# Paced loads, smaller |w| sums, one shift product per step and a reordered prologue in a kernel with a 256-step recurrence

## What is computed

```python
def cell(h, x):                              # scanned over the 256 steps
    gi = x @ W_ih + b_ih
    gh = h @ W_hh + b_hh
    r = sigmoid(i_r + h_r)
    z = sigmoid(i_z + h_z)
    n = tanh(i_n + r * h_n)
    return (1.0 - z) * n + z * h
...
x = x + moe(gru(cond, x))                    # 8 experts of 192, the best 2 per token
...
scale, shift = split(cond @ W_emb + b_emb)   # adaptation of the attention's input
xn = rms_norm(x, g) * (1.0 + scale) + shift
...
gamma = mean(abs(w))                         # of each of w1, w2, w3 (1408 x 512)
wq = clip(round(w / (gamma + eps)), -1, 1)
```

## Time and profile before

| what | value |
|---|---|
| median of 3 runs | 1829.79 us (1825.73 to 1830.11) |
| the profiled execution's own time | 1830.81 us |
| its span, first to last instruction | 1828.9 us |
| mean granted TensorE clock | 0.891 |
| TensorE busy (matmul) | 1611.4 us, 88% |
| VectorE busy | 1174.7 us, 64% |
| ScalarE busy | 916.3 us, 50% |
| GpSimd busy | 599.9 us, 33% |
| DMA moved | 90.36 MB |
| of it instructions, queues q8 and q14 | 3.83 MB in 234 packets, 0.66 MB in 81 |

### The profile page before, as it was taken

How to read it: one execution, slowest core, us unless ns; L and a number is a source line. 1 busy time by engine, 2 the same in 40 slices (tenths; PEclk the granted TensorE clock), 3 DMA queues, 4 the chain that set the end, 5 groups by cost and what they waited for, 6 DMA issues and landing times. The chain is left out here.

```text
span 1828.9 us, 77444 instructions
## 1 busy us (share of the span) xinstructions
PE 1611.4 (88%) x32043; PEld 1223.2 (67%) x32043; DVE 1174.7 (64%) x4229; ACT 916.3 (50%) x3325; POOL 599.9 (33%) x1805
## 2 busy tenths in 40 slices
PE   6999999999999999896299965788888888699999
PEld 5988999889999998896266532354545555444444
DVE  5777877777787788777644436566565666474231
ACT  5545555445455555545245445367666667532130
POOL 0333333323333333334345444133223223580000
PEclk9999999999999999555599985789888989699999
DMA  6010010200000001202446444000000000040001
GB/s 239 5 49 30 5 52 5 98 33 5 5 4 5 5 22 56 76 22 73 134 138 238 133 169 137 1 2 0 0 0 0 0 0 1 12 128 18 29 1 47
DMA packets 30635, 90.36 MB, mean 49 GB/s; under 512 B 4848, under 2 KB 6000, under 8 KB 30192
## 3 DMA queue, kind: packets, MB, share of 16 engines
q1 hardware_dynamic: 23920, 64.88, 10.4%
q0 software_dynamic: 6400, 20.98, 3.4%
HBM read 66.90 MB, written 18.87 MB: 47 GB/s over the span
## 5 line engine op out<-in xcount | busy, mean ns | idle before, releaser
L363 PE MATMUL bank<-arena 128*128 128x8 f16 x12288 | 500.9, 170 | 25.2 <-issue 14.0
L366 PE MATMUL bank<-arena 128*128 128x16 f16 x12288 | 495.2, 182 | 2.7 <-issue 2.1
L363 PEld LDWEIGHTS bank<-arena 128*128 128x128 f16 x12288 | 414.4, 97 | 57.9 <-ACT bank L459 32.0
L366 PEld LDWEIGHTS bank<-arena 128*128 128x128 f16 x12288 | 411.9, 97 | 4.1 <-issue 3.2
L635 POOL TENSOR_TENSOR arena<-arena 128x16 f32<-128x16 f32 x512 | 116.8, 228 | 565.9 <-DVE arena L566 551.2
L429 ACT ACTIVATE arena<-arena 128x16 f32<-128x16 f32 x512 | 114.4, 223 | 327.4 <-DVE arena L545 327.3
L545 DVE TENSOR_REDUCE arena<-bank 128x16 f32<-128x48 f32 x512 | 99.5, 194 | 105.2 <-PE bank L366 102.4
L556 DVE TENSOR_TENSOR_SCAN arena<-arena,bank 128x64 f32<-128x64 f32 x512 | 146.7, 287 | 21.0 <-ACT arena L429 6.9
L1898 PE MATMUL bank<-arena 128*128 128x512 f16 x704 | 152.3, 379 | 1.7 <-PEq L1419 1.7
L336 PE MATMUL bank<-arena 128*128 128x256 f16 x1008 | 150.4, 277 | 0.8 <-issue 0.7
L1454 PE MATMUL bank<-arena 128*128 128x512 f16 x576 | 144.4, 406 | 4.5 <-DVE arena L1698 4.5
(11 more groups left out here) (201 smaller groups left out, 2699.9 us busy)
## 6 DMA issues: line engine op xcount, KB each, us to landing
arena<-yrows SPq DMA_DIRECT2D x16, 512.0 KB, 4.1
arena<-in_wgu SPq DMA_DIRECT2D x8, 768.0 KB, 4.7
hrows<-arena SPq DMA_DIRECT2D x16, 256.0 KB, 4.1
arena<-in_xtok SPq DMA_DIRECT2D x16, 256.0 KB, 8.0
out_y<-arena SPq DMA_DIRECT2D x16, 256.0 KB, 2.0
arena<-in_wih SPq DMA_DIRECT2D x4, 768.0 KB, 7.5
arena<-in_whh SPq DMA_DIRECT2D x4, 768.0 KB, 5.3
arena<-in_xT SPq DMA_DIRECT2D x3, 1024.0 KB, 5.9
```

The costliest lines, as they stand in the source:

```text
L363: mm = nc.tensor.matmul(dst[:, j * B:(j + 1) * B, 1], w, h[:, 0], start=home not in opened, stop=False, skip_group_check=True)
L366: mm = nc.tensor.matmul(dst[:, j * B:(j + 1) * B, 1:3], w, h.rearrange("p a c -> p c a"), start=home not in opened, stop=False, skip_group ...
```

## The change

- SyncE's loads within the recurrence are cut: x in pieces of 128 KB (one k of one window of 32 steps), the quarters of w1, w2, w3 in twelve pieces of 176 KB, the experts' gate and up weights in parts of 128 KB, W_emb in sixteen pieces of 128 KB. Before each piece SyncE waits for the count of one more step's r sum (`r_pre[0]`), so that one piece goes out per step, in steps that the program names. From the nineteenth part of the experts' weights on, the wait is for the split of the part eighteen before.
- The splits of x move from steps 0 to 4 of a window to steps 16 to 20.
- The sums of |w| are 48 of 352 elements instead of 24 of 704, in twelve successive steps from 34, 66, 98 and 130. The first quarters are loaded within the recurrence and no longer ahead of it.
- The shift products are taken k by k, one per step, in the last 32 steps; half of W_emb gets a place of its own (8 KB a partition), the other half stays over x. `adapt` moves behind `thresholds` in the second block.
- Prologue: x and the first weight slice are loaded ahead of the six small tensors and split first; for the first ten tiles TensorE takes the two products with the weight's high half as soon as that exists, then waits for the low half.

```diff
-        ABS_AT = {first + 4 * i: (c, i) for c, first in enumerate((9, 41, TC + 9, 2 * TC + 9)) for i in range(6)}
+        HI_AT = {16: 0, 17: 1, 18: 2, 19: 3}
+        LO_AT = {17: 0, 18: 1, 19: 2, 20: 3}
+        ABS_AT = {first + i: (c, i) for c, first in enumerate((34, 66, 98, 130)) for i in range(3 * ABS)}
...
+                def load_x(c, first):
+                    if c > 1:
+                        sp.wait_ge(x_lo, (c - 1) * KT)
+                    for k in range(KT):
+                        if c > 1:
+                            sp.wait_ge(r_pre[0], first + k)
+                        sp.dma_start(xc[:, k, half_of(c)], xT[:, k, bass.ts(c, GC)]).then_inc(x_in[c % 2], 16)
...
+                def load_abs(c, first):
+                    n = WN // P // NCH // ABS
+                    if c > 0:
+                        sp.wait_ge(wal_used, 3 * ABS * c)
+                    for i in range(3 * ABS):
+                        w, part = (w1f, w2f, w3f)[i // ABS], i % ABS
+                        sp.wait_ge(r_pre[0], first + i)
+                        sp.dma_start(wal[:, i // ABS, part * n:(part + 1) * n], w[:, bass.ts(c * ABS + part, n)])\
+                            .then_inc(wal_in, 16)
+
+                load_x(0, 0)
+                load_weight(0)
                 sp.dma_start(cst[:, :], consts).then_inc(small_in, 16)
...
+                for i in range(1, 2 * KT):
+                    load_weight(i)
+                load_x(1, 0)
+                load_x(2, 6)
+                load_abs(0, 10)
+                load_x(3, 30)
+                load_abs(1, 50)
+                load_x(4, 64)
+                load_abs(2, 82)
+                load_x(5, 98)
+                load_abs(3, 114)
+                load_x(6, 128)
+                for n in range(3 * PARTS):
+                    sp.wait_ge(r_pre[0], 134 + n)
+                    load_raw_part(sp, n)
+                load_x(7, 154)
+                sp.wait_ge(x_lo, NGC * KT)
+                for k in range(KT):
+                    for i in range(4):
+                        sp.wait_ge(r_pre[0], 182 + 4 * k + i)
+                        sp.dma_start(wel[k][:, i * 2 * P:(i + 1) * 2 * P], wemb[:, k, i * 2 * P:(i + 1) * 2 * P])\
+                            .then_inc(we_in, 16)
+                for n in range(3 * PARTS, NGU * PARTS):
+                    sp.wait_ge(pw_lo, n - 3 * PARTS + 1)
+                    load_raw_part(sp, n)
...
                         pe.wait_ge(x_lo, k + 1)
+                        pe.wait_ge(w_hi, k + 1)
+                        for mt in range(n_first):
+                            b, half = FIRST_SLOTS[mt]
+                            for xp in range(2):
+                                nc.tensor.matmul(bank[b][:, half_of(half)], wihs[:, 0, k, mt, :], xs[:, xp, k, half_of(0)],
...
                         pe.wait_ge(w_lo, k + 1)
...
-                    i = t - (NCH - 1) * TC - SHIFT0
-                    if 0 <= i < 8 * KT // SHIFTS:
-                        for n in range(SHIFTS * i, SHIFTS * i + SHIFTS):
-                            shift_part(n)
+                    if t >= SHIFT0:
+                        shift_part(t - SHIFT0)
...
+                act.wait_ge(consts_done, 1)
+                A.activation(fn[:, 0, 3:4], ones[:, 0:1], ACT.Sigmoid)
+                for k in range(KT):
+                    high_x(0, k)
+                high_w(0)
                 act.wait_ge(small_in, 6 * 16)
...
+                for k in range(KT):
+                    low_x(0, k)
+                low_w(0)
                 dve.wait_ge(small_in, 6 * 16)
...
                 thresholds()
+                adapt()
```

More of the change, by code:

```diff
@@ L25 @@
 TG = GC // B
+ABS = 4
 G3 = 3 * D
@@ L166, in raw_piece, with raw_count, load_raw_part @@
             return raw3[0:parts, n % 3, 0:src.shape[1]]
+        def raw_count(n):
+            return 16 * sum(PARTS if i < NGU else 1 for i in range(n % 3, n + 1, 3))
+        def load_raw_part(sp, n):
+            at = n * PART
+            sp.dma_start(raw_part(n), wgu[:, at:at + PART]).then_inc(raw3_in[n // PARTS % 3], 16)
         def load_piece(sp, n):
@@ L189, in mixed_net_kernel @@
         wihs = m.take([2, KT, GM, P], F16)
-        wel = Mem(arena, m.at).take([KT, 2 * D], F32)
+        wel01 = Mem(arena, m.at).take([2, 2 * D], F32)
         xc = m.take([KT, CH], F32)
@@ L236, in mixed_net_kernel @@
         raw_in = [sem(f"raw_in{i}") for i in range(4)]
-        x_in = sem("x_in")
+        x_in = two("x_in")
         wal_in = sem("wal_in")
@@ L265, in _ @@
                 sp.dma_start(wrf[:, :, :], wr).then_inc(small_in, 16)
[L266 to L277, removed]
@@ new lines, in _ @@
+                for k in range(KT):
[6 more added lines that the diff above has]
+                    load_raw_part(sp, n)
+                for n in range(NGU, NGU + 3):
@@ L306, in project_x @@
                         pe.wait_ge(x_lo, k + 1)
+                        pe.wait_ge(w_hi, k + 1)
[3 more added lines that the diff above has]
+                                nc.tensor.matmul(bank[b][:, half_of(half)], wihs[:, 0, k, mt, :], xs[:, xp, k, half_of(0)],
+                                                 start=(k == 0 and xp == 0 and half == 0), stop=False,
+                                                 skip_group_check=True)
                         pe.wait_ge(w_lo, k + 1)
@@ L309, in project_x @@
                             b, half = FIRST_SLOTS[mt]
[L310 to L313, removed]
+                            mm = nc.tensor.matmul(bank[b][:, half_of(half)], wihs[:, 1, k, mt, :], xs[:, 0, k, half_of(0)],
+                                                  start=False, stop=(k == KT - 1), skip_group_check=True)
                             if k == KT - 1:
@@ L407, in _ @@
                 A.activation(mv[:, 1, 0, :, 2], h0, ACT.Copy, scale=SX).then_inc(h_init, 1)
[L408 to L421, removed]
+                for i in range(1, 2 * KT):
+                    high_w(i)
                 for k in range(KT):
@@ L515, in _ @@
                                     None, ALU.mult)
[L516 to L519, removed]
                 dve.wait_ge(h_init, 4)
                 V.tensor_tensor(mv[:, 1, 1, :, 2], inh[:, :, 2], mv[:, 1, 0, :, 2], ALU.subtract).then_inc(h_init, 1)
[L522 to L536, removed]
+                for i in range(1, 2 * KT):
+                    low_w(i)
                 for k in range(KT):
@@ L913, in turn_back @@
                     mm.then_inc(turn_mm, 1)
-                nc.tensor.matmul(bank[6][:, 0:6 * NCH], ones[:, :], gsum.rearrange("p c w a -> p (c w a)"),
+                nc.tensor.matmul(bank[6][:, 0:3 * ABS * NCH], ones[:, :], gsum.rearrange("p c w a -> p (c w a)"),
                                  start=True, stop=True).then_inc(gam_mm, 1)
```

94 lines of the change are left out of this document (52 added, 42 removed).

## The result

The changed kernel takes 1806.74 us, the median of 4 runs (1805.89 to 1809.11); the kernel before, in the same job, 1829.95. The ratio is 0.9881, 95% interval 0.9864 to 0.9898: faster by 1.2%, some 22 us. The forecast was 1799 with a range of 1790 to 1812, so it holds, with 8 us of the forecast gain missing. A repetition of the unaltered changed kernel in a later job gave 0.9900 (0.9875 to 0.9926), which puts the gain at 18 to 22 us.

A forecast was written before the change was run, and what follows sets the result against it. TensorE, busy nine tenths of the recurrence, was taken as the bound, disturbed by late instructions behind load bursts. Terms -15.5 + 2.5 - 7.4 - 5.9 - 4.1 + 0.3 = -30.1 us, taken as 31: 1799, range 1790 to 1812.

The forecast's parts named there:

- Bursts and holes: Recurrence: load bursts delay TensorE's instructions; loads in pieces, one per step, remove 15.5 us of holes and low-clock time.
- my sign was 1: Sign of being right: no hole above 1 us, and issue waits before the recurrent matmuls together under 6 us.
- the holes stay: Rival: instruction supply is late by itself or not the holes' cause; only 17.1 us go, 1813; chance 0.08.
- Small holes: Recurrence: of 5.2 us in many small holes, half, 2.5 us, was taken to go with the bursts.
- my count by steps: Recurrence: 224 steps at 3.025 and 32 at 3.044 would be 775 us, some 33 less than measured.
- Cost of the pieces: Recurrence: the 136 paced pieces themselves delay instruction supply, 2.5 us added; bounds nothing to 19 us.
- The rival of 0.1 us per piece: Rival: each of 136 pieces in the recurrence costs 0.1 us, 14 us in all, time 1810; chance 0.17.
- the rival that ends slower: Rival: a fixed price per piece meeting instruction fetch; at 0.3 us each, 41 us, time 1837; chance 0.04.
- Sums, products: Recurrence: smaller sums of abs(w) on VectorE save 7.4 us; one shift product per step on TensorE saves 5.9 us.
- The term of -4.1 us: Prologue: x and first weight loaded first move ScalarE's chain to the first step 4.1 us earlier; bounds 1 and 4.9.
- a first step after 31 us: Sign of being wrong, in the prologue; the first step was expected near 29.5 us.
- Adaptation: Four small VectorE operations moved from the recurrence to before the first router sum: 0.3 us added, bounds 0 and 0.9.

The follow-up runs named there:

- e11: Changed kernel with its loads as whole transfers and without SyncE's waits for the count of steps; ratio 0.9950 to the kernel before.
- e12: The changed kernel once more, unaltered, to measure scatter; ratio 0.9900 to the kernel before.
- e6: Changed kernel with 60 load pieces fewer, so nothing is loaded from step 22 to 133; ratio 0.9880 to the kernel before.
- e8: Changed kernel with three further pieces of 176 KB behind each of 72 paced pieces, 216 more; ratio 1.0003 to the kernel before.
- e4: Changed kernel with its sums of abs(w) as before, 24 of 704 elements; ratio 0.9917 to the kernel before.
- e5: Changed kernel with two shift products per step in 16 steps from 230 on, as before; ratio 0.9912 to the kernel before.
- e3: Changed kernel with the same small pieces but without SyncE's waits for the count of steps; ratio 0.9906 to the kernel before.
- e1: Changed kernel with the old prologue (small tensors first, then x and the weights); ratio 0.9890 to the kernel before.
- e2: Changed kernel with four of ScalarE's twelve reads of first projections moved ahead of its last weight copy; ratio 0.9870 to the kernel before.
- e9: Changed kernel with four reads ahead of the last weight copy and ScalarE's second-window x copies behind the first step's staging; ratio 0.9883 to the kernel before.

## Why the prediction was right, and where not

*Bursts and holes: right.* The big holes were data bursts delaying TensorE's instructions: none above 1.1 us is left (my sign was 1), and e11 brings them back elsewhere. The issue waits before the recurrent matmuls are 4.9 us, under the 6 that I had named, but 9.6 in e12. The rival "the holes stay" falls.

*Small holes: one step failed.* I let half of the 5.2 us of small holes go ("I take half, 2.5"). The small ones were 16.8 - 10.9 = 5.9 us before and are 6.2 after and 12.9 in the repetition. In e6 the 112 steps without loads have 3.3 us of them, as the changed kernel's have 3.0, and e6's holes too end 2.2 to 2.8 us after an instruction packet's start. So they don't need data in flight, and nothing shows that taking the bursts away shortens them. The same scatter is why my count by steps, from 16 lucky steps of 3.025, gave 33 us and made me raise 30.1 to 31: it should not have. The recurrence gave 807.4 - 783.9 = 23.5 us; the parts alone had 26.3. (By the trace of e12 it gave 9.5, in an execution 7 us above its median.)

*Cost of the pieces: not measurable.* I put in 2.5 us; e6 shows none, but couldn't show so little. If it is nothing, this and the small holes cancel. The rival of 0.1 us per piece holds for the three further pieces of e8, not for the first of a step, and the rival that ends slower has its point there: with four times the data per step (e8) the whole gain is gone.

*Sums, products: right.* 352 elements take 0.51 us (forecast 0.52) and lengthen no step; the last steps are 3.07 us (forecast 3.04) with one product each. 7.4 and 5.9 us stand, within what e4 and e5 can tell: of the 8.1 us that the last 31 steps gave, 2.8 are the hole at 743.89, which leaves 5.3 for the products.

*Prologue: wrong.* The term of -4.1 us is the one that failed, at the sentence that the chain of ScalarE's copies and reads "moves by the 2.8" and more. It moved hardly: ScalarE's last weight copy started at 25.78 before and at 25.15 after, 0.6 us earlier, and I had not asked what TensorE would wait for once it was early. The answer is in ScalarE's program order, with a wait of 5.25 us and a fallen clock. The first step at 34.65 is my own sign of being wrong ("a first step after 31 us"). The second step starts at 40.0 in the trace of before and at 40.0 to 42.9 in those with the new order: 0 in place of -4.1, or a little worse. In the two traces the forecast's 31 us came out as 24.2 (1828.9 - 1804.7): the recurrence gave 2.8 less than its parts, the extra 0.9 had nothing behind it, the prologue cost 0.9 where 4.1 were to go, and what follows the recurrence was 1.7 shorter where 0.3 more was forecast, which is luck. The result has 23.2 us. Why the last slice of W_hh landed no more than 0.6 us earlier, though it was issued 1.7 us earlier (17.77 against 19.42) and the loads of w1 to w3 were gone, wasn't tried.

*Adaptation:* what follows the recurrence took from 982.8 to 987.0 us over all traces (986.2 before, 984.5 after); 0.3 us can't be seen in that.

## What to carry to other kernels

Where TensorE runs hundreds of small matmuls back to back, its own instructions are a stream that shares the DMA engines: look for idle time inside a group of matmuls with no releaser, see what was queued some 6 to 10 us before, and spread loads over steps, small and one at a time. Before crediting an earlier start, follow each engine's program order to the next thing that the early one will wait for; in the traces, four reads moved ahead of a weight copy gave 1.4 us and more, the whole new order of loads by itself nothing. And when terms are differences of a few microseconds, take a second profile of the same kernel first: here it moved the sum of small holes from 6.2 to 12.9 us.

## What the runs showed of the hardware that I had not expected

- Cutting transfers into small ones removes the long holes even with nothing paced: 5.6 MB issued within 28 us (from 379 us on) in pieces left holes of at most 1.1 us (e3), in whole transfers two of 2.35 and 1.87 (e11).
- TensorE has small holes of up to 0.8 us with no data transfer under way: eight, 3.3 us in sum, in 112 steps of e6.
- The same 24 projection matmuls took 2.79 us behind a wait of under 1 us (before, e1, e2, e9) and 4.16 to 5.30 behind one of 3.1 to 5.3 us, where the granted clock fell to its low level (the ten traces with the changed kernel's prologue). The small recurrent matmuls hardly notice the clock: 24 of them took 0.74 us at a granted clock of 1.00 (before, at 33.73) and 0.79 at 0.50 (e2, at 32.20).
